# The second attention layer of an eight-batch transformer, rewritten from a looped bfloat16 form into straight code with float32 scores

## The reference, cut to what matters

```python
def _L1_attn_ref(x, Wq, Wk, Wv, Wo, bo):      # 16 heads of 8 numbers
    q = (x @ Wq.T).reshape(B, T, H, D).transpose(0, 2, 1, 3)
    ...
    s = jnp.einsum('bhtd,bhsd->bhts', q, k) / scale
    m = jnp.max(s, axis=-1, keepdims=True)
    e = jnp.exp(s - m)
    num = jnp.einsum('bhts,bhsd->bhtd', e, v)
    den = jnp.sum(e, axis=-1, keepdims=True) + EPS
    out = (num / den).transpose(0, 2, 1, 3).reshape(B, T, H * D)
    return out @ Wo.T + bo
```

## Time and profile before

| | us |
|---|---|
| median of 3 runs (5381.23 to 5394.14) | 5383.95 |
| profiled execution, its own time | 5385.47 |
| its span, first to last instruction | 5381.8 |
| PE busy | 4441.0 (83%) |
| DVE busy | 3600.3 (67%) |
| ACT busy | 2434.8 (45%) |
| POOL busy | 2517.5 (47%) |

### The profile page before, as it was taken

How to read it: one execution, slowest core, us unless ns; L and a number is a source line. 1 busy time by engine, 2 the same in 40 slices (tenths; PEclk the granted TensorE clock), 3 DMA queues, 4 the chain that set the end, 5 groups by cost and what they waited for, 6 DMA issues and landing times. The chain is left out here.

```text
span 5381.8 us, 169918 instructions
## 1 busy us (share of the span) xinstructions
PE 4441.0 (83%) x70369; PEld 2813.2 (52%) x70369; DVE 3600.3 (67%) x6107; ACT 2434.8 (45%) x3020; POOL 2517.5 (47%) x3540
## 2 busy tenths in 40 slices
PE   3556557677777999799988999889988999889997
PEld 2333322232224666466655666556665666556664
DVE  6655665566655777577756777567766777567774
ACT  2434434334444554355544555345543555445553
POOL 2000011111116777177744777267763777357770
PEclk9778867777889999899989999899999999899998
DMA  0000000000003222122221222022221222123220
GB/s 28 0 0 0 0 1 0 0 0 0 0 0 82 74 75 69 31 76 77 76 54 46 72 77 77 26 74 78 72 68 37 75 73 78 41 56 80 73 73 16
DMA packets 156800, 247.15 MB, mean 46 GB/s; under 512 B 33488, under 2 KB 50896, under 8 KB 155472
## 3 DMA queue, kind: packets, MB, share of 16 engines
q1 hardware_dynamic: 156240, 238.09, 16.6%
HBM read 20.38 MB, written 2.10 MB: 4 GB/s over the span
## 5 line engine op out<-in xcount | busy, mean ns | idle before, releaser
L1089 ACT ACTIVATE ls_r<-PS 128x1024 f32<-128x1024 f32 x192 | 196.6, 1024 | 883.9 <-PE PS L967 883.9
L1168 DVE TENSOR_TENSOR ls_a<-PS,TC 128x1024 f32<-128x1024 f32 x384 | 467.6, 1219 | 123.0 <-ACT ls_r L1089 123.0
L1178 DVE TENSOR_REDUCE ls_ss<-ls_r 128x16 f32<-128x1024 f32 x384 | 466.2, 1214 | 97.1 <-ACT ls_r L1114 97.1
L870 POOL TENSOR_TENSOR ls_a<-ls_a,ls_q 128x1024 f32<-128x1024 f32 x192 | 452.9, 2359 | 114.5 <-DVE ls_q L1173 114.5
L385 POOL TENSOR_TENSOR QT<-MXT,ONE 3x512 bf16<-3x512 bf16 x128 | 147.1, 1149 | 739.2 <-ACT MXT L538 732.0
L1173 DVE TENSOR_TENSOR ls_q<-PS,TS 128x512 f32<-128x512 f32 x768 | 491.1, 680 | 0.0
L890 POOL TENSOR_TENSOR ls_a<-ls_a,ls_q 128x1024 f32<-128x1024 f32 x192 | 456.2, 2376 | 0.0
L1024 PE MATMUL PS<-WO,ls_r 128*128 128x128 f32 x3072 | 404.2, 286 | 58.6 <-ACT ls_r L1117 58.6
L1024 PEld LDWEIGHTS PS<-WO,ls_r 128*128 128x128 f32 x3072 | 367.2, 196 | 105.0 <-ACT ls_r L1117 105.0
L657 DVE TENSOR_REDUCE mxs<-PS 128x1 f32<-128x512 f32 x512 | 329.1, 687 | 133.0 <-PE PS L420 126.2
L967 PE MATMUL PS<-WQ,ls_xsT 128*128 128x512 f32 x768 | 389.7, 631 | 11.8 <-ACT ls_xsT L1072 6.8
(11 more groups left out here) (217 smaller groups left out, 9363.7 us busy)
## 6 DMA issues: line engine op xcount, KB each, us to landing
ls_vb<-ls_vt SPq DMA_DIRECT2D x1152, 130.0 KB
ls_vb<-ls_vt SPq DMA_DIRECT2D x672, 65.0 KB
ls_xs<-XL SPq DMA_DIRECT2D x42, 256.0 KB, 2.3
WQ<-wqkv SPq DMA_DIRECT2D x6, 1536.0 KB, 6.4
ls_vb<-ls_vz SPq DMA_DIRECT2D x96, 65.0 KB
WO<-wo SPq DMA_DIRECT2D x24, 128.0 KB, 6.1
X<-x SPq DMA_DIRECT2D x8, 256.0 KB, 5.3
out<-X SPq DMA_DIRECT2D x8, 256.0 KB, 3.5
```

What stands on the lines that cost most here:

```text
L870: pool.tensor_tensor(a4[:, 1], a4[:, 1], b4[:, 1], ALU.add).then_inc(s_ck, 1)
L1168: nc.vector.tensor_tensor(v4(A[fq])[:, a], src, tab, ALU.mult).then_inc(done, 1)
L1178: nc.vector.tensor_reduce(ss[:, fq, a * H:a * H + H], v4(SQ)[:, a], AX.X, ALU.add).then_inc(done, 1)
```

## The change

The function `attention` serves the first attention alone. Its branches for the second are gone; its own instructions are the same, and stand in the same order. The buffers `mxs`, `MXS`, `MXT`, `ONE`, `V2` and rows 96 to 98 of `KT` leave the first phase, with their memsets; those that stay are set to zero by GpSimd beside the second layernorm. `sqs` has its own memory.

The second attention is new code, unrolled in Python for all batches. Its unit is a slot `t`, 16 tiles `k` long. There are 32 groups of four heads and 36 slots. A group takes the heads js, js+4, js+8 and js+12, one from each quarter of 32 rows. q and k are made transposed in one float32 matmul each, and the 32 rows of a quarter hold four heads; GpSimd makes four masked copies of k (`KZ`), in each of which only one head of each quarter is not zero. So a score tile is one float32 matmul over the 32 rows of a quarter.

In slot t, tile k issues: one tile of maxima scores of group t (L684, row quarter k mod 4, three PSUM banks), one tile of transposed scores of the group before, shifted by 4 tiles (L693, float32, row quarter k+2 mod 4, three banks), and a bfloat16 matmul of ones with the maxima's three parts (L694) into the same bank and quarter. Between these stand, at fixed k, the transposes of the maxima of group t-1 (k = 2), the value sums of group t-2 (k = 4, 6, 8, 10), one item of the next batch's preparation (k = 5), the last batch's output transposes and projection (k = 9), and the transposes of the sums (k = 13). ScalarE takes one 128 x 512 exponential a tile; GpSimd adds the residual.

```diff
-                                if not first:
-                                    for g in range(NG):
-                                        pool.wait_ge(s_me, b * NG + g + 1)
-                                        for i in range(GH):
-                                            pool.tensor_tensor(QT[MROW:MROW + 3, GH * g + i, :], MXT[PAD * i:PAD * i + 3, :],
...
+                GROUPS = B * NG
+                TILES = NT * GH
+                LAG = TILES + 4
+                SLOTS1 = GROUPS + 4
...
+                def later(t, k):
+                    m = TILES * t + k - LAG
+                    s, i = m // TILES, m % TILES
+                    return m, s, i // GH, (i + 2) % GH
...
+                    for t in range(SLOTS1):
+                        b, j = t // NG, t % NG
+                        for k in range(TILES):
+                            if t < GROUPS:
...
+                                if n >= 3:
+                                    pe.wait_ge(s_mx, n - 2)
+                                pe.matmul(PS[:, n % 3, :], QT[rows(g), b % 2, cols_(it)], KZ[rows(g), b % 2, j, :],
+                                          start=True, stop=True).then_inc(s_mp, 1)
+                            m, s, kt, g = later(t, k)
+                            if 0 <= m < GROUPS * TILES:
+                                p, js = (s // NG) % 2, s % NG
+                                if m % TILES == 0:
+                                    pe.wait_ge(s_me, s + 1)
+                                if m >= 3:
+                                    pe.wait_ge(s_ex, m - 2)
+                                pe.matmul(PS[:, 3 + m % 3, :], KZ[rows(g), p, js, cols_(kt)], QT[rows(g), p, :], start=True, stop=False)
+                                pe.matmul(PS[:, 3 + m % 3, :], ONE[rows(g), :], MXT[rows(g), s % 2, :],
+                                          start=False, stop=True).then_inc(s_sc, 1)
+                            if k == 2 and 0 <= t - 1 < GROUPS:
+                                pe.wait_ge(s_ms, t)
+                                claim(s_me, t)
...
+                            if k in (4, 6, 8, 10) and 0 <= t - 2 < GROUPS:
...
+                                for g in range(GH):
+                                    ins = pe.matmul(PS[rows(g), 6, :], V2[:, p, kt, GH * g + js, :], PT[:, s % 2, g, kt, :],
+                                                    start=(kt == 0), stop=(kt == NT - 1), skip_group_check=True)
+                                ins.then_inc(s_pv, 1)
+                            if k == 5 and b + 1 < B:
+                                prep(*prepared(t))
...
+                @block.scalar
...
+                                act.activation(PT[:, s % 2, g, kt, :], PS[:, 3 + m % 3, :], ACT.Exp, scale=scale).then_inc(s_ex, 1)
+                            if k == 3 and 0 <= t - 1 < GROUPS:
+                                act.wait_ge(s_mt, t)
...
+                                act.activation(MXT[:, (t - 1) % 2, :], PS[:, 7, :], ACT.Copy).then_inc(s_me, 1)
...
+                @block.gpsimd
...
+                        for j in range(NG):
+                            pool.tensor_tensor(KZ[:, b % 2, j, :], KR[:, :], mk[:, j:j + 1].to_broadcast([P, T]), ALU.mult).then_inc(s_kz, 1)
```

More of the change, by code:

```diff
@@ new lines, in scores @@
+                            def scores(h):
+                                if h >= 2:
+                                    pe.wait_ge(s_ex, b * H + h - 1)
+                                base = 3 * (h % 2)
+                                for jt in range(NT):
+                                    n = T - jt * P
+                                    o = PS[:, base + (0, 1, 2, 1)[jt], (0, 0, 0, 3 * P)[jt]:]
+                                    pe.matmul(o[:, 0:n], KT[0:KS, h, jt * P:jt * P + P], QT[0:KS, h, jt * P:T], start=True, stop=False)
+                                    ins = pe.matmul(o[:, 0:P], identb[:, :], trib[:, :], start=False, stop=True)
+                                ins.then_inc(s_sc, 1)
@@ L454, in values @@
                                     at, q0 = keys(jt)
[L455 removed]
+                                    ins = pe.matmul(PS[PAD * i:PAD * i + PAD, 6, q0:T], V1[:, jt, h % NV0, :],
                                                     PT[:, h % PTN, at:at + T - q0], start=(jt == 0), stop=(jt == NT - 1),
@@ L611, in _ @@
+                            link(nc.vector.tensor_tensor(q4, q4, wide(rot[:, 0, :, :], HD), ALU.mult))
+                            link(nc.vector.tensor_tensor(q4, q4, a4, ALU.add))
                             both = lambda z: [z[:, :, a * H:(a + 1) * H, :] for a in range(2)]
-                            parts(both(q4 if first else qk), both(q4), split).then_inc(s_spl, 1)
+                            parts(both(q4), both(q4), split).then_inc(s_spl, 1)
                             dve.wait_ge(s_spl, b + 1)
@@ L633, in outputs @@
                                 den, rc = o[:, :, :, hv], rec[:, g % 2, :, :]
-                                if not first:
-                                    link(nc.vector.tensor_scalar(rc, den, 1e-8, None, ALU.add))
-                                    den = rc
                                 link(nc.vector.reciprocal(rc, den))
-                                h0 = GH * g if not first else GH * (g % 2)
+                                h0 = GH * (g % 2)
                                 yo = Y[:, :, h0 * hv:(h0 + GH) * hv].rearrange("p t (h e) -> p t h e", e=hv)
                                 rw = rc.unsqueeze(3).to_broadcast([P, NT, GH, hv])
-                                if first and g >= 2:
+                                if g >= 2:
                                     link(nc.vector.tensor_tensor(yt[:, :, :, :], o[:, :, :, 0:hv], rw, ALU.mult))
```

429 lines of the change are left out of this document (264 added, 165 removed).

## The result

The kernel as changed takes 5727.65 us (median of 4 runs, 5705.37 to 5734.77), against 5384.54 for the kernel before in the same runs: 1.063 times as long, 95% interval 1.0604 to 1.0657. The forecast was 5339, and the range ended at 5600. The profiled execution of after took 5721.14 us, its span is 5717.7.

The account below looks back on a forecast made before the run. Bound before by turns: a serial head, then hand-overs between PE, DVE and POOL; afterwards by PE. 30 slots at 26.1 us (783) plus ends 85 give 868 us, 45 under 913: 5339 us, range 5190 to 5600.

Parts of the forecast that it names:

- The stages before and after should not move by more than 10 us: Sign for the code outside the attention stage, 4472 us, taken to keep its time.
- Rival D: Attention stage: something else is late, such as straight-line code fetch; slot 27 to 28 us, no change; 0.10 with a little of B.
- The clock: Attention stage: mean granted clock 0.96, 8% of the time at 1.2 GHz, making a slot 26.1 us.
- rival B: Attention stage: PE's waits at the slot's turn lower the clock and undo the gain; 5427 to 5928 us; chance 0.25.
- The slot at the full clock: Attention stage: PE's summed work for one group of four heads, 25.1 us, against 12 for DVE.
- rival C: Attention stage: row quarters take turns, steps of 1.93 us, slot 42 us, 5820 us in all; chance 0.08.
- The step of 0.86: Attention stage: one step of maxima, scores and ones on PE takes 0.86 us, 13.8 us for 16.
- O behind S: Ones matmul follows the scores in their quarter; with PE's in-order stream the next maxima start with it, giving 0.86 us.
- rival A: Attention stage: more overlap, steps of 0.63 us, slot 21.4 us, 5193 us in all; chance 0.20.
- The added wait: Slot's turn: a group's first score waits for ScalarE's copy of the maxima, 2.5 us against 0.86, costing 1.7 us.
- The ends: Attention stage: first preparation, first two slots and last slots outside the 30 full ones, together 85 us.
- DVE idle before L657 of some 400 us with PE named: Sign in the attention stage: VectorE's reductions wait some 400 us for PE, which is the bound.

Follow-up runs that it names:

- experiment 2: Kernel before, padded with 133 more TensorE instructions that do nothing, in the second layernorm: 5552.43 us, 1.0298 times before.
- a_first: Kernel as changed, padded, with ScalarE's copy of the maxima moved ahead of the exponential of k = 3: 5191.98 us, 0.9639 times before.
- a_defer: Kernel as changed, padded, with the ones matmul and its wait for the copy issued one step later, behind the next scores: 5187.9 us, 0.9628 times before.
- a_lag6_opposite: Kernel as changed, padded, scores two steps later (LAG = TILES + 6), head order keeping maxima and scores in opposite row quarters: 5167.72 us, 0.9574 times before.
- experiment 5: Kernel as changed, scores two steps later (LAG = TILES + 6), which also put them in the maxima's row quarter: 6247.64 us, 1.1576 times before.
- experiment 10: Kernel as changed, padded, with the ones matmul over all 128 rows: 5598.55 to 5886.62 us in four runs, 1.0456 times before without the last.

## Why the prediction was wrong

- **"The stages before and after should not move by more than 10 us": this step failed.** The forecast missed by 389 us (5727.65 against 5339): 315 of them are in the local layers, and 67 in the attention stage (935 against 868). The sum took the 4472 us outside the stage as fixed because their code is the same. The code was the same, but not its place. Rival D did name "code fetched as straight line", but priced it inside the stage and at no change. A row to suspect it was there: the local layers' loops had 55 us of stops named issue in before (L952, L1001). The [0.24 <-issue] of the earlier trace rows is no such sign; it is the pace of the weight loads there, 0.43 less 0.19 us. Nothing in the trace of before gives the size, though; only padding before (experiment 2) would have.
- **The clock: rival B came true, the size of the term was wrong.** Expected a mean of 0.96, measured 0.78 over the stage. B's mechanism was described rightly, a stop at the slot's turn for the maxima's copy, with a fall that lasts. I had read the rows at 0.62 and 0.50 as what idle PE brings, and then taken a PE with almost no idle time as safe. a_first shows that the one stop of 0.8 us in a slot made the difference: 0.78 to 0.96 on the same work, and a_defer and a_lag6_opposite, which take the stop away by other means, are at 0.94 and 0.96. The Trainium skill (TensorE: Matmul & The Clock Gate, A second HAM failure mode) tells of short idles between groups of matmuls, at PSUM banks, that make the clock go up and down; this trace agrees with it on the short idle, 0.80 us, which is here a wait for a copy. The stop is not the only thing that lowers the clock: in experiment 5, with PE busy 1444 of 1454 us and maxima and scores in turn in one quarter, it is 0.58, and in experiment 10, with PE busy 1162 of 1195 us, 0.77. (The 19% at the lower level from which B decides is 20% by the prediction's own formula; nothing hangs on it.)
- **The slot at the full clock: 25.1 us expected, 22.1 in after and 20.7 in a_lag6_opposite.** The quarters do run side by side, as chosen against rival C. The step of 0.86 was wrong, and its reason too: O behind S does not hold the next step: after each full-array piece the next M and S start 0.95 us ahead of O. The sum had them in the order of the stream, for which the prediction also cited the Trainium skill (TensorE: Matmul & The Clock Gate, Part 3, The mechanism); between row quarters this trace does not agree (second L684 at 1327.06, first L694 at 1328.01). That is the mechanism of rival A (21.4 us a slot, 5193 us), and a_first, which has it without B, took 5192. Between two groups of values a step took 0.64 us (1.29 for two, 1327.04 to 1328.33), 0.22 less than the 0.86 of the chain of one O per step. Over 16 steps that would be 3.5 us, an estimate, since not all steps run in such pairs; the slot of 22.1 us is 3.0 shorter than the sum. That a_first comes within 2 us of A's figure is in part luck: A's sum still holds the added wait of 1.7 us a slot, and no loss of clock.
- **The added wait: 1.7 us expected.** PE's weight loads waited 51.1 us for L772, 1.6 a slot; PE itself stood 0.8. From one score tile's start to the next it is 2.51 us at the turn (1108.35 to 1110.86), as the sum had it (2.5). The length was right, what it sets off was not in that term.
- **The ends: 85 us expected.** The sum counts 30 full slots beside them; 707 us of a_lag6_opposite less 30 slots of 20.7 leave 86, with the first slots at the lower clock as assumed. Right.
- **"DVE idle before L657 of some 400 us with PE named"** was 504. That PE stays the bound, and that DVE's and ACT's work hides, was right.

Taken together: the stage came out at about before's length since two errors, 3 us a slot too much and a clock of 0.96 too high, went against each other; the total went wrong by a term that was not in the sum.

## What to carry to other kernels

When a change adds or removes thousands of instructions ahead of a hot loop, its price includes the loop's new place: look for idle time named "issue" at fixed instructions of the loop, count instruction packets, and try padding of an idle engine before judging the change. Where the clock falls once in each round, look for a short stop just ahead of it and who causes it; here the order of two instructions on ScalarE was worth 202 us of the whole. And when a shift changes which heads or banks meet (LAG), write out which resources pair up before reading a mechanism from the result.

## What the runs showed that was not expected

- The place of a loop's code alone changed this kernel by up to 334 us (5727.65 to 5393.96). The kernel before took 5384.97, 5384.54 and 5552.43 us at places 100, 36 and 169. The three stops shown for after are 2.0 to 2.2 us each. They are waits for code: an instruction packet had started less than 1 us before 104 of 105 of them.
- Four row quarters of float32 scores start within 0.02 us and finish two steps in 1.3 us, where the sum had 1.7. The order of the code is not kept between quarters: a step's maxima start ahead of the ones matmul of the step before.
- The mean granted clock can be 0.56 to 0.58 with TensorE busy nearly all the time, when maxima and scores share a row quarter and take turns. In opposite quarters, without a stop for the copy, they kept 0.96.
- Less work can cost: leaving out 512 ones matmuls brought 61 short stops for VectorE and lowered the mean clock from 0.96 to 0.88, and the kernel got 18 us slower.
